# SyncE fetches ten side tiles per layer, with byte offsets worked out in the setup

## The chip, the cores and the metric

The kernel runs on one core of a Trainium2 chip. The metric is the time of one execution on the device in microseconds (us). Beside three timed executions there is one profiled execution, from which all rows below come. Engines are named as the profile names them: PE is TensorE, DVE is VectorE, ACT is ScalarE, POOL is GpSimd, SP is SyncE; SPq is SP's own sequence of instructions, which are not counted as busy time.

## The reference

Four graph layers run one after the other on a graph of 6250 nodes and 100000 edges, sorted by destination; every layer reads rows of 128 numbers by the source of an edge and adds them up by its destination.

```python
edge_index = jnp.stack([src, dst])
h = jnp.maximum(_layernorm(x, axis=-1), 0.0)
x = x + _L0_gnn_ref(h, src, dst, weight, b)              # mean of (h @ W)[src], self loops
h = jnp.maximum(_layernorm(x, axis=-1), 0.0)
x = x + _L1_gnn_ref(h, W1, W2, b1, b2, edge_weight, src, dst)   # sum of h[src] * edge_weight
h = jnp.maximum(_layernorm(x, axis=-1), 0.0)
x = x + _L2_gnn_ref(h, edge_attr_128, ..., src, dst)     # sum of (h @ Wn)[src] * net(edge_attr)
h = jnp.maximum(_layernorm(x, axis=-1), 0.0)
x = x + _L3_gnn_ref(h, edge_index, ...)                  # 4-head attention over the sources
```

## The kernel before

**Tiles and groups.** The sorted edges are cut into 782 tiles of 128, four tiles to a group, 196 groups. For every layer the node rows stand in a table in device memory (T0 with 129 numbers a row, T1 and T2 with 128, T3 with 133). An edge loop (`edge_loop` for layers 0 to 2, its own code for layer 3) brings the source rows of each tile into one of 32 places of the ring `work`, which holds eight groups, and PE multiplies each place by a mask that DVE builds from the destinations, which sums them by node.

**Who fetches.** POOL gathers a tile with one indirect DMA (`gather_groups`, L683), one table row to each partition. Before group g it waits until group g - 8 is free (L680). In seven groups of a layer, listed in `SIDE_AT`, POOL gathers three tiles only; the fourth, a **side tile**, is SP's. SP fetches its 128 rows one at a time over earlier groups: `fetch_rows` (L715 to L731) loads five row numbers into registers (L640 in `numbers`), issues one small DMA for each from the table to a side buffer (L728), and, when 64 numbers are used up, asks for the piece of 64 after next (`read_sources`, L713). Two groups after a side tile's last row, `place_rows` (L737) copies the buffer into the ring. At L728 a register holds the row's number; SP turns it into an offset with one FUSED_REGOPS, which multiplies by the row's length and by four.

**What sets the order on SP.** `relay_groups` is SP's loop, one turn a group, written out without branches. In turn n it loads four numbers of `closing` if n is a multiple of four (L640), then in `ready(n + ahead)` waits for the gathers of a later group and tells PE, DVE or ACT that they are there (L762), then fetches rows, then waits until PE or its like has used group n and raises the count that frees it for POOL (L781). In layer 2 it also loads a pair of groups of the edge network's output every second turn (L752). So an instruction that is slow in the row fetches holds up both signals behind it: L781, for which POOL waits, and the next turn's L762.

**Beside it.** ACT, PE and DVE work through the edge network in layers 0 and 1, node updates come at the end of each layer, and the setup (x, constants, the first table T0, the control tables made from sorted destinations by DVE at L402 to L513) comes before layer 0's loop. In the setup, SP's stores of T0 are L357, and L516 stores a table of windows.

Of the kernel before, what the change touches and what calls it, by code (L numbers as in the profile page):

```python
# [6 lines left out]

F32 = mybir.dt.float32
I32 = mybir.dt.int32
ALU = mybir.AluOpType  # L10
ACT = mybir.ActivationFunctionType
AX = mybir.AxisListType
ENG = mybir.EngineType

N, E, D = 6250, 100000, 128
P = 128
# [10 lines left out]
QUAD = 4  # L27
# [1 line left out]
GROUPS = -(-E // GRP)  # L29
TILES = GROUPS * QUAD  # L30
RING = 8
SIDE, SIDE_PER, SIDE_READ = 7, 5, 64
SIDE_BEGIN = [-(-(P * j) // SIDE_PER) for j in range(SIDE + 1)]
SIDE_AT = [SIDE_BEGIN[j + 1] + RING + 2 for j in range(SIDE)]
BANKS = 2
# [22 lines left out]
ROW3 = HEADS + D + 1  # L58
# [47 lines left out]
def need(engine, *marks):  # L106

    for sem, value in marks:
        engine.wait_ge(sem, value)


def build(nc, a, out):
    with ExitStack() as ctx:
# [6 lines left out]
        def dram(name, shape, dt=F32):  # L120
            return nc.dram_tensor("d_" + name, shape, dt, kind="Internal").ap()

        pe, dve, act, pool, sp = nc.tensor, nc.vector, nc.scalar, nc.gpsimd, nc.sync
        V = Lane(dve, sem("v_done"))
# [41 lines left out]

        winB, slotB = sb("winB", [1, TABB], I32), sb("slotB", [1, TABB], I32)
        needB, closingB = sb("needB", [1, TABB // QUAD], I32), sb("closingB", [1, GROUPS], I32)
# [4 lines left out]
        rn = sb("rn", [P, 2, NT])  # L173
# [20 lines left out]
        T0, T1, T2, T3 = dram("T0", [NP, D + 1]), dram("T1", [NP, D]), dram("T2", [NP, D]), dram("T3", [NP, ROW3])  # L194
        scores = dram("scores", [NP, 2 * HEADS])
        windows_b = dram("windows_b", [1, TABB])


        ld_c, ld_w = Load("ld_c"), Load("ld_w")
# [14 lines left out]
        ld_t = Load("ld_t")  # L214
# [13 lines left out]

        ld_g.add(sp.dma_start(lastg, a["lastg"]))
        ld_g.add(sp.dma_start(lastrow, a["lastrow"]))  # L230
        ld_c.add(sp.dma_start(cst[:], a["consts"]))
        steps = hT[:, 4 * TABB:5 * TABB]
        ld_c.add(sp.dma_start(steps, a["steps"].to_broadcast([P, TABB])))
        ld_t.add(sp.dma_start(rawdst, a["dsts"]))
        ld_t.add(sp.dma_start(idx, a["idx"]))
        ld_l.add(sp.dma_start(lastb, a["lasts"].to_broadcast([P, ROWS])))
        ld_t.add(sp.dma_start(wgt, a["wgt"]))
        for k, name in enumerate(("w0", "w1", "w2", "wnT", "we1T", "we2T", "wf1T", "wf2T")):
# [144 lines left out]
        st_0, dv0, nm0 = Load("st_0"), {}, {}  # L383
# [52 lines left out]
        V.did(dve.tensor_scalar(closing2[:], closing2[:], 1, None, ALU.arith_shift_right))  # L436
        V.did(dve.tensor_scalar(ctl3[:, 0:STEPS + 1, 3], slot_s, float(QUAD * ACC3), None, ALU.mult))
        need(dve, ld_t.mark)
        tables = V.did(dve.tensor_copy(dstf, rawdst))


# [82 lines left out]
        prepared = V.did(dve.memset(bcol[:, 7:8], 0.5))  # L524
# [113 lines left out]
        def numbers(engine, view, values, lo, top):  # L638

            _, v = nc.values_load_multi_w_load_instructions(  # L640
                view, engines=[engine], min_val=lo, max_val=top,
                skip_runtime_bounds_check_because="made on the chip from the sorted dst, bounded by the staircase's shape")
            assert len(v) == values
            return v
# [53 lines left out]
        def side_rows(layer, j):  # L698

            lo, width = (MLP + 11 * GRP, ACC3) if layer < 3 else (0, ROW3)  # L700
            return (acc if layer < 3 else work[:, RING * QUAD * ROW3:])[:, lo + j % 2 * width:lo + (j % 2 + 1) * width]

        def side_sources(layer, c):

            row = acc[0:1, NT * ACC3:XC] if layer < 3 else work[0:1, (RING * QUAD + 2) * ROW3:]
            return row[:, c % 2 * SIDE_READ:(c % 2 + 1) * SIDE_READ].bitcast(I32)
# [3 lines left out]

        def read_sources(layer, c):

            sp.dma_start(side_sources(layer, c), a["sides"][0:1, c * SIDE_READ:(c + 1) * SIDE_READ])\  # L713
                .then_inc(s_src[c % 2], 16)

        def fetch_rows(layer, table, n):

            width = table.shape[1]
            for c in range(SIDE_READS):
                lo, hi = [min(max(SIDE_PER * m - SIDE_READ * c, 0), SIDE_READ) for m in (n, n + 1)]  # L720
                if lo == hi:
                    continue
                if lo == 0:
                    sp.wait_ge(s_src[c % 2], 16 * (SIDE_READS // 2 * layer + c // 2 + 1))
                found = numbers(ENG.SP, side_sources(layer, c)[:, lo:hi], hi - lo, 0, N - 1)
                for r, row in zip(range(c * SIDE_READ + lo, c * SIDE_READ + hi), found):
                    j, p = divmod(r, P)
                    sp.dma_start(side_rows(layer, j)[p:p + 1, 0:width], table[bass.ds(row, 1), :])\  # L728
                        .then_inc(s_row[layer][j % 4], 16)
                if hi == SIDE_READ and c + 2 < SIDE_READS:  # L730
                    read_sources(layer, c + 2)  # L731
# [824 lines left out]
            return over  # L1556


        over = edge_loop(0, T0, [st_0.mark, ld_t.mark], [st_0.mark, ld_t.mark, prepared, tables])
        for e in (pe, dve, act, pool, sp):  # L1560
            need(e, *over)

# [1 line left out]
        over = edge_loop(1, T1, [st_1.mark], [st_1.mark, cleared[0]])  # L1564
# [15 lines left out]
        over = edge_loop(2, T2, [st_2.mark], [st_2.mark, cleared[1]])  # L1580
# [451 lines left out]
```

## Time and profile before

| | us |
|---|---|
| median of three timed runs | 5319.39 |
| lowest, highest | 5316.58, 5325.49 |
| span of the profiled execution | 5348.7 |

The profiled execution's own time isn't among the three; its span, from the first to the last instruction, is 29 us longer than their median. The span holds four edge loops, from about 85 to 1275 us, 1310 to 2530, 2595 to 3830 and 3920 to 5215, and shorter stretches between and around them. A window of the span given as 150 to 1200 is a stretch of layer 0's loop in which all that is described above repeats group by group.

### The profile page before, as it was taken

The numbers are of one execution on the slowest core, as the hardware profiler recorded it, in microseconds if no ns is written. First come the engines' busy times: TensorE is split into PE (matmuls) and PEld (weight loads), VectorE is DVE, ScalarE is ACT, GpSimd is POOL, SyncE is SP. The second block draws the span as 40 slices with busy tenths as digits, with TensorE's granted clock in tenths as the row PEclk, the third lists the DMA queues.
The fourth block names the chain that finished last, engine by engine and source line by source line (L and its number), as shares of the span: only waits on it lengthen the run. The fifth ranks groups of instructions, "written<-read, shape, count | busy, mean of one in ns | idle before, by whom it ended". The sixth has DMA issues, their size and how long they took to land. (4 is left out here: it accounts for less than half of the span.)

```text
span 5348.7 us, 68713 instructions
## 1 busy us (share of the span) xinstructions
PE 2667.0 (50%) x13316; PEld 2230.9 (42%) x13316; DVE 2614.4 (49%) x7231; ACT 1816.7 (34%) x4182; POOL 2997.4 (56%) x3172
## 2 busy tenths in 40 slices
PE   2555555544455555555333333333555555555557
PEld 1444444443344444445333333333444444444446
DVE  3333333333455555546333333333456667767678
ACT  2333333311233333312111111112345555656555
POOL 4556565555556555556355565555345555555553
PEclk7777777766777777767655565656667777767779
DMA  5333333322233333322222222223272111111110
GB/s 113 93 98 100 89 99 97 91 66 54 81 98 91 97 97 90 98 66 56 73 80 82 86 86 82 85 82 87 70 135 48 42 42 42 42 42 42 42 44 25
DMA packets 241787, 405.91 MB, mean 76 GB/s; under 512 B 67715, under 2 KB 140572, under 8 KB 241373
## 3 DMA queue, kind: packets, MB, share of 16 engines
q0 software_dynamic: 99456, 206.27, 15.7%
q10 hardware_dynamic: 74432, 122.18, 8.2%
q1 hardware_dynamic: 67484, 73.06, 4.8%
q8 instruction: 123, 2.02, 0.2%
q14 instruction: 292, 2.38, 0.1%
HBM read 331.63 MB, written 67.78 MB: 75 GB/s over the span
## 5 line engine op out<-in xcount | busy, mean ns | idle before, releaser
L683 POOL DMA_INDIRECT t_work<-d_T,t_tabG x3100 | 2926.8, 944 | 2183.9 <-SPq L781 1098.6
L1367 PE MATMUL ps<-t_work,t_acc 128*128 x2592 | 493.7, 355 | 647.6 <-SPq L762 459.1
L1367 PEld LDWEIGHTS ps<-t_work,t_acc 128*128 128x128 f32 x2592 | 440.9, 258 | 727.1 <-issue 726.7
L1428 DVE TENSOR_TENSOR t_acc<-t_acc,ps 128x128 f32 (+1 forms) x732 | 210.6, 288 | 914.8 <-remote 459.0
L1804 PE MATMUL ps<-t_work,t_hT 128*128 x1960 | 394.5, 363 | 339.0 <-ACT t_hT L1792 157.9
L1417 DVE TENSOR_TENSOR t_hT<-t_work,ps 128x512 f32<-128x512 f32 x244 | 167.2, 685 | 763.7 <-ACT ps L1504 615.0
L1804 PEld LDWEIGHTS ps<-t_work,t_hT 128*128 128x128 f32 x1960 | 337.5, 260 | 406.1 <-issue 406.1
L1367 PE MATMUL ps<-t_hT,t_acc 128*128 128x128 f32 x1296 | 275.2, 399 | 434.6 <-DVE t_acc L1428 313.0
L1504 ACT COPY ps<-t_acc 128x512 f32 x244 | 140.5, 588 | 1022.2 <-SPq L762 723.9
L596 ACT ACTIVATE t_acc<-ps,t_bcol 128x1024 f32<-128x1024 f32 x98 | 109.1, 1113 | 1079.6 <-DVE ps L609 587.4
L1367 PEld LDWEIGHTS ps<-t_hT,t_acc 128*128 128x128 f32 x1296 | 259.5, 306 | 452.6 <-DVE t_hT L1417 295.8
L1367 PE MATMUL ps<-t_work 128*128 x1312 | 247.8, 354 | 323.9 <-SPq L762 212.0
L1714 DVE TENSOR_TENSOR t_hT<-t_work,ps 128x128 f32<-128x128 f32 x980 | 270.9, 281 | 282.6 <-issue 178.6
L1367 PEld LDWEIGHTS ps<-t_work 128*128 128x128 f32 x1312 | 222.6, 258 | 364.6 <-issue 364.5
L1814 DVE SCALAR_TENSOR_TENSOR t_acc<-t_acc,t_hT,ps 128x129 f32 x980 | 336.9, 344 | 68.4 <-remote 56.3
L1726 PE MATMUL ps<-t_cst,t_hT 128*128 128x128 f32 x980 | 204.3, 344 | 249.0 <-DVE t_hT L1714 123.8
L563 PE MATMUL ps<-t_acc,t_wts 128*128 128x512 f32 x392 | 283.1, 864 | 78.8 <-DVE t_acc L602 41.1
L1777 ACT ACTIVATE t_hT<-t_hT 128x128 f32<-128x128 f32 x980 | 310.0, 390 | 0.0
L1792 ACT COPY t_hT<-ps 128x512 f32<-128x512 f32 x245 | 144.3, 589 | 464.7 <-remote 373.1
L572 PE MATMUL ps<-t_wts,t_acc 128*128 128x128 f32 x1568 | 265.4, 341 | 41.0 <-DVE t_acc L617 23.5
L1734 ACT ACTIVATE t_hT<-ps,t_hT 128x128 f32<-128x128 f32 x980 | 273.9, 359 | 32.4 <-remote 31.0
L572 PEld LDWEIGHTS ps<-t_wts,t_acc 128*128 128x128 f32 x1568 | 257.9, 257 | 45.4 <-issue 45.3
(189 smaller groups left out, 4469.0 us busy)
## 6 DMA issues: line engine op xcount, KB each, us to landing
d_edge_net<-t_acc ACTq DMA_DIRECT2D x98, 512.0 KB
t_acc<-d_edge_net SPq DMA_DIRECT2D x98, 512.0 KB
t_work<-d_T,t_tabG POOLq DMA_INDIRECT x3100
t_acc<-in_edge_attrT ACTq DMA_DIRECT2D x96, 512.0 KB
t_acc<-d_T SPq DMA_DIRECT2D x1792, 0.5 KB
t_acc<-d_T SPq DMA_DIRECT2D x896, 0.5 KB
t_work<-d_T SPq DMA_DIRECT2D x896, 0.5 KB
t_acc<-d_T ACTq DMA_DIRECT2D x12, 790.1 KB
```

What stands on the lines that cost most here:

```text
L563: last = pe.matmul(ps[:, 4 + h, :], WE1, ein[n % 2][:, h * GRP:(h + 1) * GRP], start=True, stop=True)
L572: last = pe.matmul(ps[:, 6 + k // QUAD, k % QUAD * D:(k % QUAD + 1) * D], sp1[:, k * P:(k + 1) * P], WE2, start=True, stop=True)
L683: pool.indirect_dma_start(out=work[:, at:at + width], out_offset=None, in_=table, in_offset=bass.IndirectOffsetOnAxis(ap=idx[:, g * QUAD + ...
L1367: last = pe.matmul(sums(layer, s, width), masks[s % MASKS][:, k, :], rows_k, start=(k == 0), stop=(k == QUAD - 1))
L1417: dve.tensor_tensor(out=scaled_rows[s % MASKS].rearrange("p (k d) -> p k d", k=QUAD), in0=ring[:, bass.ds(slot, QUAD * ACC3)].rearrange("p ...
L1428: dve.tensor_tensor(out=o, in0=o, in1=sums(layer, s, width), op=ALU.add).then_inc(e_acc[layer], 1)
L1714: ins = dve.tensor_tensor(out=tw[n % 2][:, k * P:(k + 1) * P].rearrange("p (h n) -> p h n", h=HEADS), in0=slots3[:, bass.ds(slots[k], HEAD ...
L1726: last = pe.transpose(ps[:, PT + n % 2, k * P:(k + 1) * P], tw[n % 2][:, k * P:(k + 1) * P], ident)
L1734: last = act.activation(ex[n % 3][:, k * P:(k + 1) * P], ps[:, PT + n % 2, k * P:(k + 1) * P], ACT.Identity, bias=ads[:, QUAD * n + k:QUAD ...
L1777: last = act.activation(e, e, ACT.Exp, bias=run[:, 0, c0 + k:c0 + k + 1], scale=1.0)
L1804: last = pe.matmul(out_of(n, k), pw[n % 2][:, k * P:(k + 1) * P], slots3[:, bass.ds(slots[k] + HEADS, ACC3)], start=True, stop=True)
L1814: dve.scalar_tensor_tensor(out=o, in0=o, scalar=corr[:, n % RINGB, k:k + 1], in1=out_of(n, k), op0=ALU.mult, op1=ALU.add).then_inc(s_add, 1)
```

## The change

The number of side tiles goes from seven to ten a layer (`SIDE`), and SP fetches seven rows a group for five (`SIDE_PER`). `SIDE_AT` goes from 36, 62, 87, 113, 138, 164, 190 to 29, 47, 65, 84, 102, 120, 138, 157, 175, 193. The row numbers are no longer read from the input but from a small table in device memory, `side_at`, with a line for each row length: in the setup DVE multiplies the numbers by the length of a row in bytes, three times, and SP stores the products. At the row fetch the table is seen as bytes, and the register holds the offset itself.

```diff
-SIDE, SIDE_PER, SIDE_READ = 7, 5, 64
+SIDE, SIDE_PER, SIDE_READ = 10, 7, 64
...
+        side_at = dram("side_at", [3, SIDE * P], I32)
...
+        side_tab = rn[:].rearrange("p j t -> p (j t)")[:, 0:4 * SIDE].bitcast(I32)
+        ld_k, st_k = Load("ld_k"), Load("st_k")
...
         ld_t.add(sp.dma_start(idx, a["idx"]))
+        ld_k.add(sp.dma_start(side_tab[:, 0:SIDE], a["sides"]))
...
         need(dve, ld_t.mark)
+        need(dve, ld_k.mark)
+        for k, width in enumerate((D + 1, D, ROW3)):
+            m_side = V.did(dve.tensor_scalar(side_tab[:, (k + 1) * SIDE:(k + 2) * SIDE], side_tab[:, 0:SIDE],
+                                             float(4 * width), None, ALU.mult))
+        need(sp, m_side)
+        st_k.add(sp.dma_start(side_at.rearrange("k (p j) -> p k j", j=SIDE),
+                              side_tab[:, SIDE:4 * SIDE].rearrange("p (k j) -> p k j", j=SIDE)))
...
-            sp.dma_start(side_sources(layer, c), a["sides"][0:1, c * SIDE_READ:(c + 1) * SIDE_READ])\
+            k = (layer + 1) // 2
+            sp.dma_start(side_sources(layer, c), side_at[k:k + 1, c * SIDE_READ:(c + 1) * SIDE_READ])\
...
-            width = table.shape[1]
+            row = 4 * table.shape[1]
+            table_b = table.rearrange("n w -> (n w)").unsqueeze(0).bitcast(U8)
...
-                found = numbers(ENG.SP, side_sources(layer, c)[:, lo:hi], hi - lo, 0, N - 1)
-                for r, row in zip(range(c * SIDE_READ + lo, c * SIDE_READ + hi), found):
+                found = numbers(ENG.SP, side_sources(layer, c)[:, lo:hi], hi - lo, 0, (N - 1) * row)
+                for r, at in zip(range(c * SIDE_READ + lo, c * SIDE_READ + hi), found):
                     j, p = divmod(r, P)
-                    sp.dma_start(side_rows(layer, j)[p:p + 1, 0:width], table[bass.ds(row, 1), :])\
+                    sp.dma_start(side_rows(layer, j)[p:p + 1, :].bitcast(U8)[:, 0:row], table_b[:, bass.ds(at, row)])\
...
-        over = edge_loop(0, T0, [st_0.mark, ld_t.mark], [st_0.mark, ld_t.mark, prepared, tables])
+        over = edge_loop(0, T0, [st_0.mark, ld_t.mark], [st_0.mark, ld_t.mark, st_k.mark, prepared, tables])
```

The order of SP's instructions at the start of layer 0's loop, one turn of `relay_groups`. ISA is the FUSED_REGOPS of the profile, t_acc holds the row numbers and receives the rows, d_T is the table; before:

```order
L640 TENSOR_LOAD t_closing
L640 TENSOR_LOAD t_acc
L728 ISA
L728 DMA t_acc<-d_T 1x129
L728 ISA
L728 DMA t_acc<-d_T 1x129
L728 ISA
L728 DMA t_acc<-d_T 1x129
L728 ISA
L728 DMA t_acc<-d_T 1x129
L728 ISA
L728 DMA t_acc<-d_T 1x129
```

The same turn and the three behind it after the change (L652 is the old L640, L742 the old L728; 516 are bytes):

```order
L652 TENSOR_LOAD t_closing
L652 TENSOR_LOAD t_acc
L742 DMA t_acc<-d_T 1x516 x7
L652 TENSOR_LOAD t_acc
L742 DMA t_acc<-d_T 1x516 x7
```

The register instruction before each row's DMA is gone, and seven DMAs stand in a turn in place of five.

Where a piece of 64 numbers ends within a turn on SP, before:

```order
L640 TENSOR_LOAD t_acc
L728 ISA
L728 DMA t_acc<-d_T 1x129
L713 DMA t_acc<-in_sides 1x64
L640 TENSOR_LOAD t_acc
```

And after:

```order
L652 TENSOR_LOAD t_acc
L742 DMA t_acc<-d_T 1x516
L726 DMA t_acc<-d_side_at 1x64
L652 TENSOR_LOAD t_acc
L742 DMA t_acc<-d_T 1x516 x6
```

Such a turn has two loads of numbers and a read of the piece after next, as before; there are more of them.

SP's setup after the change, from its last store of T0 to its first read of numbers, with what each waits for:

```order
L362 DMA d_T<-t_acc 128x129 [waits g_done,a_done] x2
L449 DMA d_side_at<-t_rn 128x3x10 [waits v_done]
L528 DMA d_windows_b<-t_acc 1x1024 [waits v_done]
L558 DMA t_acc<-in_edge_attrT 128x1024 [waits v_done]
L558 DMA t_acc<-in_edge_attrT 128x1024
L726 DMA t_acc<-d_side_at 1x64 [waits v_done,st_k,ld_t,st_0]
```

The store of `side_at` (L449) is new, ahead of the store of windows (the old L516), and the first read waits for it too.

## Rows read from the trace of the kernel before

Rows that begin with a line's name say: instruction and its tiles, how many, duration in ns (least/median/most), first and last start in us. Those of the windows say: stretch and its length, busy us and count of PE, PEld (weight loads), DVE, ACT and POOL, granted TensorE clock, share of the DMA engines, GB/s. Those of the timeline say: start, duration, engine and instruction, and in brackets the idle time before it and what ended it.

**Rows 1.** The page: busy times, and by line the chain that ended last.

```profile
PE 2667.0 (50%) x13316; PEld 2230.9 (42%) x13316; DVE 2614.4 (49%) x7231; ACT 1816.7 (34%) x4182; POOL 2997.4 (56%) x3172
...
SPq L728 8%; SPq L640 3%; PE ps L1804 1%; SPq L762 0%; DVE t_acc L1814 0%; PE ps L1944 0%; ACT t_hT L1777 0%; SPq L781 0%; DVE t_acc L1913 0%; ACT t_hT L1734 0%; DVE t_x L1976 0%; DVE t_dev L302 0%; PE ps L1726 0%; PE ps L1785 0%
```

**Rows 2.** Windows, one steady stretch in each of the four edge loops.

```profile
150.00:1200.00 1050.00, 563.84 (x2696) 456.24 (x2696) 387.92 (x661) 329.79 (x313) 625.83 (x664) 0.73 0.34 92
1450.00:2450.00 1000.00, 558.43 (x2644) 452.28 (x2645) 519.27 (x835) 316.78 (x327) 593.62 (x630) 0.73 0.31 89
2750.00:3750.00 1000.00, 361.15 (x1683) 335.41 (x1681) 333.35 (x642) 130.89 (x235) 589.87 (x626) 0.60 0.29 84
4000.00:5100.00 1100.00, 619.88 (x3268) 504.75 (x3268) 775.00 (x3303) 650.30 (x2253) 606.93 (x644) 0.76 0.20 44
```

**Rows 3.** Waits of POOL, layer 0's stretch, then layer 3's: us, times, longest.

```profile
POOL t_work L683 <- SPq L781: 212.9, 69, 4.9
...
POOL t_work L683 <- SPq L781: 313.9, 111, 5.0
```

**Rows 4.** Timeline of POOL in layer 0, idle before in brackets.

```profile
1019.97 0.94 POOL L683 DMA_INDIRECT t_work<-d_T,t_tabG  x1 [2.30 <-SPq L781]
1021.22 0.94 POOL L683 DMA_INDIRECT t_work<-d_T,t_tabG  x1 [0.30 <-issue]
...
1033.71 0.94 POOL L683 DMA_INDIRECT t_work<-d_T,t_tabG  x1 [0.30 <-issue]
1039.46 0.94 POOL L683 DMA_INDIRECT t_work<-d_T,t_tabG  x1 [4.81 <-SPq L781]
```

**Rows 5.** SP's instructions by line, layer 0's stretch; last row layer 3's L781.

```profile
L728 SPq FUSED_REGOPS  x838: 1/37/1413, 150.9 to 1197.5; - x168
L728 SPq MOVE t_acc<-d_T x838: 1/29/1452, 151.1 to 1198.9; - x168
L728 SPq DMA_DIRECT2D t_acc<-d_T x838: 2/225/1396, 151.8 to 1199.0; - x168
...
L781 SPq EVENT_SEMAPHORE  x167: 2/17/1422, 154.4 to 1193.4; - x167
...
L781 SPq EVENT_SEMAPHORE  x163: 2/17/751, 4001.6 to 5097.6; - x163
```

**Rows 6.** SP's loads of numbers, layer 0's stretch.

```profile
L640 SPq TENSOR_LOAD <-t_acc x179: 3/1072/3222, 149.7 to 1193.5; - x179
...
L640 SPq TENSOR_LOAD <-t_closing x42: 3/485/1564, 154.4 to 1179.8; - x42
```

**Rows 7.** Row fetches in POOL's pause, then beside its gathers.

```profile
L728 SPq MOVE t_acc<-d_T x4: 3/29/29, 1037.1 to 1038.3; - x4
...
L728 SPq FUSED_REGOPS  x5: 5/37/707, 1023.8 to 1027.8; - x5
...
L728 SPq DMA_DIRECT2D t_acc<-d_T x5: 3/28/702, 1024.2 to 1028.5; - x5
```

**Rows 8.** The last row fetch of layer 0, and the semaphore instructions behind it.

```profile
L728 SPq DMA_DIRECT2D t_acc<-d_T x1: 6/6/6, 1226.5 to 1226.5; - x1
...
L762 SPq EVENT_SEMAPHORE  x3: 251/714/720, 1227.0 to 1229.4; - x3
```

**Rows 9.** Reads of row-number pieces and placements, whole span.

```profile
L713 SPq DMA_DIRECT2D t_acc<-in_sides x42: 3/236/729, 81.9 to 3610.5; - x42
...
L737 SPq DMA_DIRECT2D t_work<-t_acc x21: 3/483/712, 286.6 to 3775.2; - x21
```

**Rows 10.** Setup: VectorE's L437, SP's L516 and L713, landing of L357.

```profile
L437 DVE TENSOR_SCALAR t_ctl<-t_acc x1: 366/366/366, 45.0 to 45.0; 1x245 int32<-1x245 int32 x1
...
L516 SPq DMA_DIRECT2D d_windows_b<-t_acc x1: 252/252/252, 77.8 to 77.8; - x1
...
L713 SPq DMA_DIRECT2D t_acc<-in_sides x2: 238/243/248, 81.9 to 82.2; - x2
...
DMA to landing us min/median/max: 5.1/8.2/9.5
```

More of the change, by code:

```diff
@@ L9 @@
 I32 = mybir.dt.int32
+U8 = mybir.dt.uint8
 ALU = mybir.AluOpType
@@ L2007 @@
         "lastg": lastg.reshape(2, P).T, "lastrow": lastg[:GROUPS].reshape(1, GROUPS),
-        "sides": np.concatenate([src[QUAD * g + QUAD - 1] for g in SIDE_AT]).reshape(1, SIDE * P),
+        "sides": np.concatenate([src[QUAD * g + QUAD - 1] for g in SIDE_AT]).reshape(P, SIDE),
         "idx": src[:TILES].T, "dsts": dst[:TILES].T, "wgt": weight[:TILES].T,
```

## The prediction

> **What bounds the kernel now.** I read the page's busy line and its chain first [rows 1]. No engine is busy more than 56% of the span (POOL), while the chain that ended last carries two lines of SP's queue on top: L728, the row fetches, and L640, the loads of numbers into registers. Next, the four stretches in which an edge loop runs steadily [rows 2]: POOL is busy 0.55 to 0.60 of each, PE at most 0.56, VectorE 0.70 in the last. So the question is what POOL waits for. Between gathers it stops for 0.30 us ("issue"), and on top of that it waits for SP's L781, the semaphore that frees a ring group: 212.9 us of layer 0's 1050 us and 313.9 of layer 3's 1100 [rows 3]. The timeline shows the shape: gathers follow each other every 1.25 us, so a group of four needs 5.0 us; then a pause of 2.3 to 4.8 us ended by L781 [rows 4].
>
> Is SP late because it waits, or because it works? The view of waits names no wait of SP in these stretches, and L781 was passed 167 times in 1050 us [rows 5], **6.29 us a group**, against POOL's 5.0. SP's sequencer never rests: SP bounds the edge loops, and 1.29 us a group is what POOL loses to it.
>
> **What SP's 6.29 us are.** A group has one load of five row numbers (median 1.07 us), every fourth group one of `closing` (0.485, so 0.12 a group) [rows 6], two semaphore instructions (0.017 each, with the step between instructions some 0.1 together) and five rows of three instructions each: FUSED_REGOPS 0.037, MOVE 0.029, DMA 0.225, 0.29 together [rows 5]. What a row takes is another matter. While POOL paused, MOVEs began at 1037.1 to 1038.3, three steps in 1.2 us: **0.40 us a row**. While gathers ran, FUSED_REGOPS began at 1023.8 to 1027.8, four steps in 4.0: **1.0 us a row**, with stalls of some 0.7 us or twice that in any of the three [rows 5, 7]. The stalls hit semaphore instructions too: three at L762 took 0.25, 0.71 and 0.72 us from 1227.0 on, after layer 0's last row fetch at 1226.5 [rows 8]. So with gathers in flight SP runs at less than half its speed, and in the pause at full speed. Clean work per group: 5 x 0.40 + 1.07 + 0.12 + 0.1 = 3.29 us. The pause takes 1.29 of it, so 2.00 was done in the 5.0 us of gathers, a rate of 0.40.
>
> **The change part by part.**
> (1) FUSED_REGOPS goes from each row; DMA and its MOVE stay (the built program still has a MOVE behind each row's DMA), and the bytes of a row are the same. Clean, that saves 0.037 and its step: 0.40 less 0.29 is 0.11 for three steps, so 0.037 + 0.037 = 0.07. The bounds of a whole row's saving are 0.037 (its bare duration) and a third of a stalled row, 0.33.
> (2) Two more rows a group: 7 x 0.33 = 2.31 clean for 5 x 0.40 = 2.00. +0.31.
> (3) The load brings seven numbers for five. Five take 1.07, 0.21 each: +0.43. By the row of four numbers it would be 0.12 each, +0.24; by the step from four numbers to five, 0.59 each, +1.17 [rows 6]. I take 0.43, from the load that is lengthened itself. The Trainium skill, "Runtime: NRT & Kernel Launch", section "Instruction fetch mechanics", gives about 200 ns for each register that such a load fills; that would make +0.40, and it speaks against this change in the same measure as the row does.
> (4) Per layer there are 200 loads of row numbers for 191 (more rows straddle the 64-number pieces), 20 reads of a piece for 14 at 0.23 us, ten placements for seven at 0.48 [rows 9]: clean some 9 x 0.25 + 6 x 0.23 + 3 x 0.48 = 5 us, or 0.03 a group. The 0.25 is what a load costs beside its values, estimated as 0.485 less two values of 0.12.
> (5) Rows are fetched in 183 groups a layer for 180: three more groups pay the pause of 1.29 us, +4 us a layer.
> (6) Three gathers fewer a layer, 3 x 1.25 = 3.75 us. POOL isn't the bound: SP lacks the 0.40 x 3.75 = 1.5 us of work that it did beside them, so 2.2 us a layer are gained. Were POOL the bound, all four layers would gain 15 us: that is the most the fewer gathers can give.
> (7) Setup: a small load, three VectorE instructions of ten columns, a store. They stand behind L437, which starts at 45.0; SP's next store, L516, starts only at 77.8 and the first read of the table at 81.9 [rows 10]. 32 us cover a store that the 5.1 to 9.5 us landings of the T0 stores bound from above [rows 10]. Nothing; without cover at most 10 us, once.
>
> **The sum, and how stalls are shared.** Clean work per group becomes 3.29 + 0.31 + 0.43 + 0.03 = 4.06 us. What remains open is how much of it SP gets done in the 5.0 us of gathers, and three readings of the stalls give three times.
> (a) Each instruction pays its own stall. Before, 15 + 1.25 + 2 = 18.25 instructions have 0.18 us of clean work each, and at the rate of 0.40 take 0.45: 0.27 of stall each. Afterwards 14 + 1.3 + 2 = 17.3 have 0.235 and take 0.505, so 9.9 pass in 5.0 us and 7.4 are left for the pause: 1.74 us, +0.45 a group.
> (b) Instructions pass at a fixed pace when gathers run, 11.1 in 5.0 us, and a longer one hides its stall. 6.2 are left at 0.235: 1.46 us, +0.17.
> The truth should lie between. For (b) speaks that the long load shows a median of 1.07 although most loads run beside gathers; for (a), that a DMA of 0.225 shows stalls of its own, up to 1.396 [rows 5]. I take the middle, **+0.31 us a group**. Over 183 groups and four layers that is +227; (5) and (6) add 4 x 2: +235. Layer 3 has a longer group, 1100/163 = 6.75 us [rows 5], so a larger share of pause, and I take the same step for it. The profiled span of 5348.7 becomes 5584; the median of the timed runs is 0.55% below that span, and carrying the difference gives 5319 + 235, about **5550 us**, 4.3% slower. With (a) alone 5650, with (b) alone 5450. A TENSOR_LOAD at either bound moves the sum by -70 or +290 us, worked the same way.
>
> **The rivals.**
> *Stalls take a share of time* (slower still). If SP simply runs at 0.40 of its speed beside gathers whatever it executes, 2.00 us are done there and 2.06 left: +0.77 a group, +572 us with (5) and (6), 5890. For it: the rate is the simplest reading of 0.40 against 1.0 us a row. Against it: bare register instructions with 0.037 of work stall as long as DMAs do.
> *FUSED_REGOPS feeds the stalls* (faster). Without it SP alternates between two kinds of instruction in a row and not three. If that halved the stall of every other instruction, from 0.27 to 0.13, 0.235 + 0.13 = 0.37 each, 13.5 pass in 5.0 us, 3.8 are left: 0.89 us of pause, -0.40 a group, about -290: 5030. It turns into a gain once the stall of the others falls below some 0.19, by 30%. For it: row instructions stall in any position. Against it: in the pause the same sequence runs without stalls, so the sequence alone causes none; and the semaphore instructions, with no register arithmetic near, stalled as well [rows 8].
> *Nothing to see.* If the loads' two further numbers cost 0.12 each and stalls go by (b), the step is +0.1 or less, and a stall or two less per group brings it to zero: 5310 to 5370.
> *The change doesn't do what it says*: the order shows FUSED_REGOPS gone from all rows, so only the MOVE could differ; I give it nothing.
>
> **How the numbers follow.** Forecast 5550 (between 5420 and 5700): 0.55. By share of time, 5760 and up: 0.15. Faster, through weaker stalls: 0.20, half of it above 5180. No difference: 0.10, of which some 0.06 within 0.2%, about what a measurement of this kernel can tell from no change. Range 5180 to 5780: it leaves out half of the faster case and most of the share-of-time case, 2 in 10 together. Faster 0.22, same 0.06, slower 0.72.
>
> **What the profile of the changed kernel would show.** Right: no FUSED_REGOPS at the row fetch and 5120 rows; the free signal passed every 6.5 to 6.8 us in layer 0; the loads of seven numbers at 1.4 to 1.6 us; POOL's waits for the free signal up from 213 us to some 260 in the same stretch; POOL's own step still 1.25 us. Wrong: the free signal at 6.2 us or below with rows at 0.5 us beside gathers (the stalls shrank); at 7 us or above (share of time); or waits of SP for PE or for landed gathers in the steady stretches, which would mean that SP no longer bounds.

## The result: 5352 us for 5320, and the profile after

The changed kernel takes 5352.4 us (median of 4 runs, 5349.2 to 5356.2); the kernel before took 5319.8 beside it (4 runs, 5316.6 to 5325.5). The ratio is 1.0063, with a 95% interval of 1.005 to 1.0077: slower, by 0.6% where 4.3% were forecast. The profiled run took 5356.2 us, its span is 5354.9.

The page of the kernel after, busy times, the chain by line, and the gathers; they answer to [rows 1]:

```profile
PE 2722.2 (51%) x13316; PEld 2286.6 (43%) x13316; DVE 2615.0 (49%) x7234; ACT 1820.7 (34%) x4182; POOL 2987.2 (56%) x3160
...
SPq L742 33%; SPq L652 19%; SPq L776 1%; SPq L795 1%; SPq L766 1%; PE ps L1381 1%; POOL t_work L695 0%; PE ps L1818 0%; DVE t_acc L1828 0%; ACT t_acc L314 0%; DVE t_acc L1927 0%; PE ps L1958 0%; SPq L726 0%; DVE t_x L1990 0%
...
L695 POOL DMA_INDIRECT t_work<-d_T,t_tabG x3088 | 2914.5, 944 | 2208.2 <-SPq L795 1122.7
```

SP's instructions by line in layer 0's stretch of 1050 us (count, least/median/most in ns, first and last start), as in [rows 5] and [rows 6]; L742 was L728, L652 was L640, L795 was L781:

```profile
L742 SPq MOVE t_acc<-d_T x1162: 2/29/1414, 151.5 to 1200.0; - x194
L742 SPq DMA_DIRECT2D t_acc<-d_T x1161: 2/228/1397, 151.6 to 1199.7; - x194
...
L652 SPq TENSOR_LOAD <-t_acc x182: 3/1466/3450, 149.0 to 1194.7; - x182
...
L795 SPq EVENT_SEMAPHORE  x165: 2/17/1411, 154.2 to 1192.5; - x165
```

POOL's waits in layer 0's stretch and in layer 3's (us, times, longest), as in [rows 3]:

```profile
POOL t_work L695 <- SPq L795: 220.3, 69, 5.3
...
POOL t_work L695 <- SPq L795: 313.3, 119, 5.4
```

FUSED_REGOPS is gone, 1161 rows pass in 1050 us where 838 did, and the load of seven takes 1.47 us. Yet the free signal comes 165 times for 167: 6.36 us a group for 6.29. POOL waits for it as often as before, 69 times, 3.2 us each for 3.1; in layer 3 nothing moved either, 313.3 us for 313.9. From start to start in the trace, layer 0's stretch, a row took 0.89 us of SP before (DMA 0.39, FUSED_REGOPS 0.25, MOVE 0.25) and 0.60 after (0.36 and 0.24). So five rows took 4.47 us, seven take 4.18; the loads of numbers took what the rows gave back, 1.57 us a group for 1.29.

### The profile page after: what moved, and what is told of

Read it like the earlier page. It is cut to its first block, busy times and chain, and to the rows that moved or that the text cites. A ratio compares the mean times of both kernels' runs of the same rounds, so it can differ in the third digit from the quotient of the medians.

```text
span 5354.9 us, 68270 instructions
## 1 busy us (share of the span) xinstructions
PE 2722.2 (51%) x13316; PEld 2286.6 (43%) x13316; DVE 2615.0 (49%) x7234; ACT 1820.7 (34%) x4182; POOL 2987.2 (56%) x3160
## 4 chain that ended last, share of the span: by engine, by line
SPq 56%; issue 30%; DVE 4%; another core or an unknown queue 3%; PE 3%; ACT 2%; POOL 1%; DVEq 0%; DMA 0%; ACTq 0%; POOLq 0%
SPq L742 33%; SPq L652 19%; SPq L776 1%; SPq L795 1%; SPq L766 1%; PE ps L1381 1%; POOL t_work L695 0%; PE ps L1818 0%; DVE t_acc L1828 0%; ACT t_acc L314 0%; DVE t_acc L1927 0%; PE ps L1958 0%; SPq L726 0%; DVE t_x L1990 0%
## 5 line engine op out<-in xcount | busy, mean ns | idle before, releaser
L1818 PE MATMUL ps<-t_work,t_hT 128*128 x1960 | 409.8, 373 | 246.1 <-issue 130.5
L1818 PEld LDWEIGHTS ps<-t_work,t_hT 128*128 128x128 f32 x1960 | 349.6, 268 | 315.0 <-issue 315.0
L1740 PEld LDWEIGHTS ps<-t_cst,t_hT 128*128 128x128 f32 x980 | 137.0, 177 | 381.7 <-DVE t_hT L1728 296.1
L584 PE MATMUL ps<-t_wts,t_acc 128*128 128x128 f32 x1568 | 276.3, 351 | 6.1 <-issue 5.5
```

The lines of the kernel that those rows point to most:

```text
L584: last = pe.matmul(ps[:, 6 + k // QUAD, k % QUAD * D:(k % QUAD + 1) * D], sp1[:, k * P:(k + 1) * P], WE2, start=True, stop=True)
L1740: last = pe.transpose(ps[:, PT + n % 2, k * P:(k + 1) * P], tw[n % 2][:, k * P:(k + 1) * P], ident)
L1818: last = pe.matmul(out_of(n, k), pw[n % 2][:, k * P:(k + 1) * P], slots3[:, bass.ds(slots[k] + HEADS, ACC3)], start=True, stop=True)
```

## The experiments

**Two kinds of chip.** Where a run lands decides more than any edit here. On three chips the kernel before takes 5262 to 5331 us (below: chips A; the 5320 beside the result is of this kind), on three others 4183 to 4187 (chips B). Every ratio is against the kernel before on the same chip.

| run | edit | chip | us | before | ratio, 95% interval |
|---|---|---|---|---|---|
| e1 | five rows, byte offsets | B | 4187.6 | 4186.9 | 1.000, 0.999 to 1.001 |
| e2 | seven rows, FUSED_REGOPS | B | 4296.0 | 4186.9 | 1.026, 1.024 to 1.028 |
| e3 | no side tiles | B | 4216.4 | 4186.9 | 1.007, 1.005 to 1.009 |
| e4 | the change, aligned loads | B | 4176.7 | 4186.9 | 0.997, 0.996 to 0.999 |
| e5 | the change again | A | 5278.7 | 5262.2 | 1.003, 1.002 to 1.005 |
| e6 | before, for its trace | A | 5282.2 | 5262.2 | one run |
| e7 | as e1 | A | 5292.8 | 5324.4 | 0.993, 0.991 to 0.996 |
| e8 | as e2 | A | 5708.7 | 5324.4 | 1.073, 1.070 to 1.075 |
| e9 | as e4 | A | 5352.4 | 5324.4 | 1.006, 1.004 to 1.008 |
| e10 | as e3 | A | 5246.2 | 5324.4 | 0.985, 0.983 to 0.988 |
| e11, e12 | the change, 2 and 4 idle instructions a gather | B | 4169.9, 4171.1 | 4183.3 | 0.997, 0.995 to 0.998 (both) |
| e13 | before, 2 of them | B | 4182.2 | 4183.3 | 1.000, 0.999 to 1.001 |
| e14, e15 | the change, 6 and 8 | A | 5331.4, 5359.1 | 5331.0 | 1.001 and 1.005, 0.9995 to 1.002 and 1.003 to 1.007 |
| e16 | before, 6 | A | 5253.1 | 5331.0 | 0.986, 0.984 to 0.988 |
| e17 | the change, gathers of 64 rows | B | 4046.5 | 4183.2 | 0.967, 0.966 to 0.969 |
| e18 | the change, gathers of 64 columns | B | 4168.5 | 4183.2 | 0.997, 0.996 to 0.998 |

**The change taken apart** (T1: each instruction brings its own stall; T2: a fixed pace or a share of time). e1 keeps the byte offsets and goes back to five rows:

```
-SIDE, SIDE_PER, SIDE_READ = 10, 7, 64
+SIDE, SIDE_PER, SIDE_READ = 7, 5, 64
```

> The changed kernel with seven side tiles and five rows a turn, as before, so only the offsets in bytes are left of the change. Theory 1 (SP's instructions bound the edge loops): a row takes 0.30 us less than before, 1.5 us of SP's time a group, of which the coupling with POOL leaves 0.6 to 0.8 us: groups of 5.5 to 5.7 us, 4740 to 4900 us in all. Theory 2 (the group's 6.3 us are set elsewhere, by landings or by what uses the ring, and SP only fills them, which is why the group stayed at 6.3 us with the change): 5300 to 5330.

e2 keeps ten tiles and seven rows, and lets SP multiply again (the table then holds row numbers, multiplied by 1.0 in the setup):

```
-sp.dma_start(side_rows(layer, j)[p:p + 1, :].bitcast(U8)[:, 0:row], table_b[:, bass.ds(at, row)])
+sp.dma_start(side_rows(layer, j)[p:p + 1, 0:width], table[bass.ds(at, 1), :])
```

> The changed kernel with ten side tiles and seven rows a turn, but with row numbers in the registers and the multiplication back at each row: the other half of the change alone. Theory 1: 0.30 us more for each of seven rows, at least a third of it on the group: 6.9 to 7.5 us a group, 5750 to 6200 us. Theory 2: about 5350.

e3 has no side tile (SIDE = 0): POOL gathers every tile, SP fetches no row.

> No side tiles: POOL gathers all 782 tiles of a layer, SP only passes signals. Theory 1: POOL's 5.0 us a group become the bound, less 1.3 us for 180 groups in four layers, plus 28 gathers at 1.25 us: 4400 to 4500 us. Theory 2: 5300 to 5400.

e4 is the change with each group's seven numbers in a slot of eight:

```
+SIDE_SLOT = 8
-found = numbers(ENG.SP, side_sources(layer, c)[:, lo:hi], hi - lo, 0, (N - 1) * row)
+found = numbers(ENG.SP, side_sources(layer, c)[:, lo:lo + many], many, 0, (N - 1) * row)
```

> The changed kernel with the seven offsets of a turn placed in eight, so that each load begins at a multiple of 32 bytes and no turn straddles a piece. Theory 1: a load of seven takes 0.9 to 1.1 us where it took some 1.5, and 17 fewer loads a layer: 0.2 to 0.5 us less a group, 5000 to 5200 us. Theory 2: 5340 to 5360.

All four landed on a chip B, where no expectation in us could hold. What they show is the kernel without stalls. SP's row instructions in e2, from 150 to 1200 us (on a chip B that is layer 0's loop to about 1050 and the start of layer 1's):

```profile
L741 SPq FUSED_REGOPS  x1327: 37/37/37, 150.0 to 1199.6; - x190
L741 SPq MOVE t_acc<-d_T x1327: 29/29/29, 150.0 to 1199.7; - x190
L741 SPq DMA_DIRECT2D t_acc<-d_T x1327: 224/225/1018, 150.1 to 1199.8; - x190
```

The longest of 1327 FUSED_REGOPS takes 37 ns; in [rows 5] it was 1413. Gathers run as densely here, or denser, so gathers alone cause no stall: it takes the chip as well. In e1 POOL is the bound, its idle time being mostly its own 0.30 us ("issue") between gathers; in e2 SP is, with 54% of the chain. The gathers of e1, then e2's chain:

```profile
L695 POOL DMA_INDIRECT t_work<-d_T,t_tabG x3100 | 2935.9, 947 | 1054.9 <-issue 904.2
```

```profile
SPq L741 29%; SPq L652 25%; POOL t_work L695 8%; DMA t_work<-d_T,t_tabG 2%; SPq L765 1%; DVE t_acc L1827 1%; PE ps L1380 1%; ACT t_acc L314 0%; DVEq L652 0%; PE ps L1957 0%; PE ps L575 0%; DVE t_acc L1926 0%; SPq L726 0%; DVE t_x L1989 0%; DVE ps L1414 0%
```

Seven rows with FUSED_REGOPS need 5.2 us a group in e2 (from the starts, layer 0), over POOL's 5.0; without it they fit. There the edit does what a reader of the code would hope.

**The same on chips A.** First the change itself and the kernel before once more:

> The changed kernel itself, unaltered, beside the kernel before on one chip. On the chip of the first four experiments the kernel before takes 4187 us, where it took 5320 beside the first run of the change. Theory A: what differs is the stalls of SyncE's instructions beside the gathers (a FUSED_REGOPS 256 ns in the trace of before, 76 ns in that of e2_7rows_regops). Where the kernel before takes near 4190, the change takes 4175 to 4205: GpSimd's 1.25 us a gather is the bound, twelve gathers fewer are worth up to 15 us, and loads of seven that are not aligned give back part of it. Where it takes near 5320, the change takes 5340 to 5365 again, a ratio of 1.005 to 1.008. Theory B (SyncE is the bound in either case, and the change adds the same work to a group): a ratio of 1.005 to 1.01 in both.

> The kernel before, unaltered, for its trace on this chip. Where it takes near 4190 us: theory A expects FUSED_REGOPS 0.07 to 0.08 us, MOVE 0.06 to 0.07 and the issue of a row's DMA 0.26 to 0.30 us from one instruction to the next beside the gathers, a group of 5.0 us, and SyncE waiting in the first loop. Theory B expects groups over 5.1 us, with GpSimd waiting for SyncE's free signal at one group in two or more. Where it takes near 5320: 0.25, 0.25 and 0.39 us as in the first trace.

The chip was an A: 1.003, a little under what was expected, and a FUSED_REGOPS of 0.24 us from start to start. Then e1 to e4 again, all on one chip A:

> The kernel of e1 once more (five rows and seven side tiles as before, byte offsets, so FUSED_REGOPS is all that goes), wanted on a chip where the kernel before takes near 5260 us. There its row takes 0.89 us of SyncE's time beside gathers (0.40 DMA, 0.24 MOVE, 0.24 FUSED_REGOPS) and in the change 0.60. Theory P (each instruction brings its own stall of some 0.17 us): 5 x 0.60 + 1.21 of loads + 0.6 of the rest = 4.8 us a group, under GpSimd's 5.0, so the free signal comes in time and the time falls to 4300 to 4500 us. Theory S (the gathers set the number of stalls, whatever SyncE executes): only the clean 0.07 to 0.09 a row go, 0.4 us a group, 4900 to 5000. Theory R (a stall merely moves to the next instruction and fills the time): 5230 to 5270. Where the kernel before takes 4187 again: 4180 to 4195.

> The kernel of e2 once more (ten side tiles and seven rows as in the change, FUSED_REGOPS as before), on the same chip as e7. Theory P: 7 x 0.89 + 1.6 of loads + 0.6 = 8.4 us a group for 6.2, some 6700 to 6900 us. Theory S: two more rows at their clean 0.42 and 0.35 more of loads, 7.4 us a group, 6100 to 6250. Theory R: 5300 to 5600. Where the kernel before takes 4187: 4290 to 4300 again.

> The kernel of e4 once more (the change, with the seven numbers of a group in a slot of eight, so that every load begins at a multiple of 32 bytes and no group needs two loads), on the same chip as e7. Its loads should take some 1.4 us for 1.6 a group. If SyncE's clean work counts in full (P and S): 5278 - 0.2 x 730 = 5100 to 5180 us. If stalls fill what the load leaves (R): 5240 to 5280. Where the kernel before takes 4187: 4174 to 4180 again.

> The kernel of e3 once more (no side tiles: GpSimd gathers every tile, SyncE fetches no rows), on the same chip as e7. If all that differs between the two chips is SyncE's stalls, the time is that of the other chip, 4210 to 4260 us, where the kernel before takes 5262, so that the row fetches cost 1000 us here. If the gathers or the other engines are slower here as well: 4400 us or more.

P (each instruction brings its stall) and S (gathers set the number of stalls) fall with e7. Five of SP's instructions a group are gone, a row takes 0.79 us for 0.89, and the kernel gains 0.7%; R (a stall moves on and fills the time) is nearest. e8 came out between R and S, and e9 (5352) above both of its ranges: aligned loads gave nothing. The run that decides is e10: SP fetches nothing, its queue idles, and the time falls by 1.5% only. Had SP's stalls been all that the two kinds of chip differ in, e10 would have come at 4210 to 4260 us; it took 5246, and e3, the same kernel on a chip B, 4216. Free signals in the stretch and POOL's waits for them, e10, e7, then e8:

```profile
L782 SPq EVENT_SEMAPHORE  x177: 17/17/17, 151.3 to 1187.5; - x177
...
POOL t_work L684 <- SPq L782: 166.8, 52, 6.1
```

```profile
L795 SPq EVENT_SEMAPHORE  x175: 2/17/1398, 155.5 to 1192.9; - x175
...
POOL t_work L695 <- SPq L795: 188.9, 65, 4.4
```

```profile
L794 SPq EVENT_SEMAPHORE  x157: 1/17/707, 150.1 to 1198.9; - x157
...
POOL t_work L695 <- SPq L794: 291.1, 90, 6.2
```

POOL waits 3.2, 2.9 and 3.2 us on average in the three, 3.1 in the kernel before and 3.2 in the change. The mean wait hardly depends on what SP has to do; what changes is how often it comes: 52, 65, 69, 69 and 90 times in e10, e7, before, the change and e8.

Who is late in e10? TensorE's timeline (start, duration, what, idle before):

```profile
994.90 1.39 PE L1368 MATMUL ps<-t_work,t_acc 128*128 x11
997.11 0.27 PE L1368 MATMUL ps<-t_work,t_acc 128*128 x1 [0.81 <-issue]
997.81 0.27 PE L1368 MATMUL ps<-t_work,t_acc 128*128 x1 [0.43 <-issue]
999.24 0.38 PE L1368 MATMUL ps<-t_work,t_acc 128*128 x1 [1.16 <-issue]
1001.37 0.60 PE L1368 MATMUL ps<-t_work,t_acc 128*128 x2 [1.75 <-issue]
1010.70 1.19 PE L564 MATMUL ps<-t_acc,t_wts 128*128 128x512 f32 x1 [8.74 <-DVE t_acc L603]
```

Eleven matmuls pass in 1.4 us, and then they come one at a time, on steps of 0.7, 1.4 and 2.1 us: SP's steps, on another engine. In this stretch SP waits in its turn; where the profile names who ended a wait of L782 it is TensorE (33 times of 87), and "remote" means that it names nobody:

```profile
SPq L782 <- remote: 731.4, 54, 23.7
SPq L782 <- PE ps L573: 106.8, 20, 6.9
```

The 8.74 us in front of the last matmul are more than a stall of TensorE. From 1001.97 to 1008.53 us the trace has no instruction of any engine but POOL, whose gathers go on; its last one before the pause ends at 1005.43, and the others go on 3.1 us later. In e10's layer 2 such standstills are longer. A window of 20.3 us (counts of PE, weight loads, DVE, ACT and POOL), then the first instructions of VectorE and POOL behind it:

```profile
3009.90:3030.20 20.30, 0.00 (x0) 0.00 (x0) 0.00 (x0) 0.00 (x0) 12.21 (x13) 0.57 0.25 71
3030.36 0.71 DVE L1429 TENSOR_TENSOR t_acc<-t_acc,ps 128x128 f32 x2 [21.64 <-remote]
3033.14 0.95 POOL L684 DMA_INDIRECT t_work<-d_T,t_tabG  x1 [7.38 <-SPq L782]
```

VectorE waited for the semaphore of a matmul that began at 3009.53; the trace has the signal at 3030.24. Whether the matmul or its signal was late, it doesn't tell. Counted in the trace, stretches of over 5 us without any instruction but POOL's, SP's included, are 23 of layer 0's 1050 us (189 us in all), 10 of 1000 us of layer 1 (91 us), 34 of 1000 us of layer 2 (546 us) and none in layer 3, whose 6.80 us a group stay unexplained. Of the 33 in layers 0 and 1, 23 end 2.9 to 3.2 us after the last gather of a run ends. e3, the same kernel on a chip B, has none in any layer. So in layers 0 to 2 of e10 it is the run of gathers that holds up the rest, and POOL then waits for what it held up. The kernel before and the change have no such stretch over 1.5 us: there SP always gets an instruction through.

**When the stalls come.** POOL's pauses in the kernel after (idle time in brackets), then SP's row fetches from 1007.2 to 1010, 1014 to 1020 and 1020 to 1022.7 us:

```profile
1007.43 0.94 POOL L695 DMA_INDIRECT t_work<-d_T,t_tabG  x1 [3.56 <-SPq L795]
1020.01 0.94 POOL L695 DMA_INDIRECT t_work<-d_T,t_tabG  x1 [2.90 <-SPq L795]
```

```profile
L742 SPq MOVE t_acc<-d_T x5: 29/29/29, 1008.4 to 1009.8; - x5
...
L742 SPq DMA_DIRECT2D t_acc<-d_T x6: 3/694/711, 1013.8 to 1018.9; - x6
...
L742 SPq MOVE t_acc<-d_T x4: 29/29/29, 1021.3 to 1022.4; - x4
```

A run of gathers starts at 1007.4. For 3 us more SP runs clean, then its DMAs take 0.7 us each. The next run starts at 1020.0, and again SP is clean at first. Over layer 0's stretch of the kernel before, from the starts in the trace, 35% of the FUSED_REGOPS stall (over 0.6 us from start to start) from 2.75 us behind a run's start to 2.75 us behind its end (the run's shadow), and 1% at other times. Within a run the share grows: of its MOVEs and FUSED_REGOPS (over 0.5 us, loops of layers 0 and 1) at most 1 in 100 stall in the first 2 us, some 3 in 10 in the fifth and sixth, some 6 in 10 from the seventh on. Loads of five numbers take 0.89 us on average within the shadow and 1.10 outside, so they show no stall on top of their own time, though single ones take up to 3.2.

The pauses fit to this. Counted from the starts in the same stretch; a pause is the step between two gathers less 1.25 us, where that is over 0.95 us:

| kernel on a chip A | gathers per pause | usual run, and its median pause |
|---|---|---|
| e10, no rows | 13.4 | 16 gathers, 3.5 us |
| e7, five rows, bytes | 10.9 | 12 gathers, 3.5 us |
| before | 8.6 | 8 gathers, 2.6 us; 12 gathers, 4.1 us |
| the change | 8.1 | 8 gathers, 2.6 us |
| e8, seven rows, FUSED_REGOPS | 7.1 | 8 gathers, 3.4 us |

A usual pause takes 0.18 to 0.34 of the run ahead of it. By the free signals a group takes 5.93 us in e10, 6.00 in e7, 6.29 before, 6.36 in the change and 6.69 in e8: SP's rows matter, but far less than their own time. That suggests a limit on the gathers themselves (theory B: they pile up, the pile stalls every sequencer, and it drains only while POOL stops).

Two things in the traces narrow B down. First, not every queue stalls. In layer 0's stretch steps of over 1.0 us between two weight loads of one line, which no kernel on a chip B shows, number 41 in e10 and 24 in e7, all in the shadow of a run, and none before, in the change and in e8, whose runs are shorter. POOL's own 167 semaphore instructions before take 0.02 us at most, and so do ScalarE's. Second, what piles up isn't the gathers' data. By the packets in the traces from 150 to 1000 us, a gather's first one starts 1.64 us behind the gather's start and its last one ends 2.2 us behind it (medians), for the first gather of a run as for the eighth, at most 5.3 us before and 5.3 in e10; on a chip B it is 1.65, 2.2 and 5.2 us (e13). Nor is it the fetching of instructions by its number: SP's row instructions before stall 572 times in the stretch, with 46 packets on one of the two instruction queues and 26 on the other. And no slower clock of TensorE explains a standstill in which it runs nothing; the granted clock was about 0.70 on chips A and 0.78 on chips B.

**Slower gathers.** To tell B from C (each gather brings its own stalls) and D (gathers have no part in it), POOL got semaphore instructions that nobody waits for behind each gather. The list `s_pace` has two; e12 runs over it twice (`s_pace * 2`), e14 and e16 three times, e15 four times:

```
                         .then_inc(GATHERED[g % RING], 16)
+                    for s in s_pace:
+                        pool.sem_inc(s, 1)
```

> The change, with two semaphore instructions on GpSimd behind every gather that nobody waits for, so that a gather takes some 1.38 us for 1.25 and a group at least 5.5 for 5.0. Wanted where the kernel before takes 5260 to 5320 us. The traces so far show SyncE's stalls of 0.7 us only from 3 us after a run of gathers begins to 3 us after it ends, and more of them the longer the run lasts. Theory B (gathers that follow each other faster than some 6.1 us a group pile up, and the pile is what stalls the sequencers): slower gathers mean fewer stalls, the share of row instructions over 0.6 us falls from 0.30 to under 0.2, and the time stays within 1% of the change's own, 5270 to 5400. Theory C (each gather brings its own stalls, whatever went ahead): the share stays at 0.3 and the group at 6.3 or more, 5300 to 5450. Theory D (SyncE's stalls have nothing to do with gathers, and GpSimd's 5.0 us hides nothing): the pause stays 1.3 us on top of 5.5, 5600 to 5750. Where the kernel before takes 4187: 4450 to 4650, since GpSimd is the bound.

> The same with four such semaphore instructions behind every gather: some 1.5 us a gather, 6.0 a group. Theory B: at that pace nothing piles up, the share of row instructions over 0.6 us falls to 0.1 or less, GpSimd hardly waits for the free signal, and a group takes 6.1 to 6.3 us: 5200 to 5400 us, about the same as without the pace although a gather takes a fifth longer. Theory C: the share stays near 0.3, the group at 6.3 to 6.6, 5300 to 5550. Theory D: 1.3 us of pause on top of 6.0, 6000 to 6150. Where the kernel before takes 4187: 4850 to 5050.

> The kernel before with the two semaphore instructions of e11. SyncE has 0.6 us less clean work a group than in the change. Theory B: fewer stalls and less work, so the group follows GpSimd at 5.6 to 6.1 us, 5000 to 5300 us, at least 1% under e11. Theory C: 6.2 to 6.4 us a group, 5300 to 5400. Theory D: 5600 to 5700. Where the kernel before takes 4187: 4450 to 4650.

These three ran on a chip B, and the gathers didn't slow down: the median step stayed 1.25 us, so the times are those of the bare kernels. The four instructions of e12 didn't fit into the 0.30 us between two gathers, as the next expectation has it; most of them ran while a gather was busy. That gives the change its time on such a chip: 4169.9 for 4183.3, 13 us faster, for its twelve gathers fewer (e3, with 28 more, is 29 us slower).

> The change with six semaphore instructions behind every gather on GpSimd. Four of them (0.078 us each in the trace of e12) fitted into the 0.30 us that GpSimd leaves between gathers, so six should make a gather 1.41 us and a group 5.6. Where the kernel before takes 5260 to 5320 us: theory B (gathers that pile up stall the sequencers) expects the share of SyncE's row instructions over 0.5 us to fall from 0.30 to under 0.2 and the time to stay within 1% of the change's own, 5270 to 5400; theory C (each gather brings its own stalls) a share of 0.3, 5300 to 5450; theory D (nothing of SyncE's work is hidden in the longer gathers) 5600 to 5750. Where the kernel before takes 4187: 3096 x 0.16 = 490 more than 4170, some 4600 to 4700.

> The same with eight semaphore instructions: 1.57 us a gather, 6.3 a group. Where the kernel before takes 5260 to 5320 us: theory B expects a share of stalls of 0.1 or less, hardly a wait of GpSimd for the free signal, and 5350 to 5500 us; theory C a share near 0.3 and 5450 to 5650; theory D 6100 or more. Where the kernel before takes 4187: 3096 x 0.31 = 970 more than 4170, 5050 to 5200.

> The kernel before with the six semaphore instructions of e14. SyncE has 0.6 us less clean work a group than in the change. Where the kernel before takes 5260 to 5320 us: theory B expects the group to follow GpSimd at 5.7 to 6.1 us, 5000 to 5300 us, and under e14 by 1% or more; theory C 6.2 to 6.4 us a group, 5250 to 5400; theory D 5600 to 5750. Where the kernel before takes 4187: 4600 to 4700.

On a chip A the times fell where B had them, but by no proof of B: POOL's queue ran ahead of its gathers, the median step between gathers stayed 1.25 us in all three, and of SP's MOVEs 28% and 23% still stalled in e14's and e15's shadow, for 31% in e5, where B wanted under 20% and 10%. e14's and e16's times suit C as well. What they do show: the stalls hit POOL's queue too, once it has many instructions beside its gathers (in e15 259 of its 5345 semaphore instructions take over 0.5 us). Its added instructions, and its waits, in e15:

```profile
L702 POOLq EVENT_SEMAPHORE  x5182: 2/17/732, 149.8 to 1199.4; - x200
...
POOL t_work L697 <- issue: 409.4, 630, 4.1
POOL t_work L697 <- SPq L799: 29.7, 17, 2.4
```

They take up to 0.73 us, where e12's, on a chip B, show:

```profile
L702 POOLq EVENT_SEMAPHORE  x3300: 17/17/17, 150.2 to 1199.9; - x195
```

In e15 POOL waits 30 us for SP in place of 220, and 409 us for its own queue, in place of 196. In e14 to e16 the runs became shorter (5.2 to 6 gathers, 1.8 us of pause), and in e15 the group is 6.36 us again, 165 free signals. With 32 more instructions a group on POOL the change takes as long as without them (1.005 for 1.003 to 1.006), and the kernel before with 24 more is 1.4% faster.

**Rows or bytes.** e17 gathers 64 of 128 rows behind the first eight groups, e18 64 of 129 columns:

> The change with every gather on GpSimd behind the first eight groups cut to its first 64 of 128 rows (the other rows keep what an earlier group left there, so the sums are others and the work of all other engines is the same). Where the kernel before takes 5260 to 5340 us: if the rows that pile up are what stalls the sequencers (theory B, by rows), the share of SyncE's row instructions over 0.5 us falls from 0.30 to under 0.1 and the group from 6.3 us to SyncE's or GpSimd's bound of 4.2 to 5.0, so 4000 to 4400 us; if each gather brings its stalls by its number alone (C), share and time stay, 5250 to 5350; if neither gathers nor their rows matter (D), 5300 as well, with the stalls also outside the shadow of the gathers. Where the kernel before takes 4187: 4000 to 4170, by what a gather of 64 rows takes on GpSimd.

> The change with every gather behind the first eight groups cut to the first 64 of its 129 columns, all 128 rows (from a view of the table with rows of 64, so the sums are others). The number of rows is the same, the bytes half. Where the kernel before takes 5260 to 5340 us: by rows (B) or by gathers (C) nothing changes, 5250 to 5360; if it is the bytes that pile up, the share of stalls falls to under 0.15 and the time to 4200 to 4700. Where the kernel before takes 4187: 4150 to 4180.

Both ran on a chip B and tell nothing of the stalls. There half the rows shorten a gather by 5% and the step by 4% (0.899 us for 0.945, a step of 1.20 for 1.25), half the bytes by nothing.

## Why the prediction was right in its sign and wrong in its size

- **"SP bounds the edge loops, and 1.29 us a group is what POOL loses to it": this step failed.** The views showed SP never at rest and POOL waiting for SP, and both are so. But without any row fetch POOL still loses 167 us of the 1050 to that wait (e10, for 213 before), or 0.94 us a group of the 1.27, and the kernel gains 1.5%. The engine waited for was busy because it was stalled, and with its work gone others were held up in its place: in e10 the whole core but POOL stands still for up to 20 us while gathers run. A sequencer full of stalls isn't full of work. Why runs of gathers do this on chips A stays open.
- **"What remains open is how much of it SP gets done in the 5.0 us of gathers": wrong question.** All three readings took a rate beside gathers and put the rest of SP's work into the pause. Against +0.77 us a group of clean work, as forecast, (a) gave +0.45, (b) +0.17, the sum +0.31; 165 signals for 167 are +0.08. From before to the change the median pause stayed 2.6 us and came after 8.1 gathers for 8.6, and the share of stalls shrinks as the work grows: 43 to 50% of the row instructions in the shadow in e7 (over 0.6 us, by kind), 36 to 41% before, 31% in the change (e5), 18 to 24% in e8. That the stalls give way to SP's work is what the prediction lacked.
- **Clean work 3.29 to 4.06 us: right in its parts.** FUSED_REGOPS was priced at 0.07 us a row; e2 has 0.076 for it from start to start, and its DMA takes 0.01 more than e4's. With stalls it took 0.25, within the 0.33 given as the bound, and five of these paid for the two further rows. The load of seven took 1.47 us for the 1.4 to 1.6 forecast, +0.39 to the load of five. (The Trainium skill, "Runtime: NRT & Kernel Launch", section "Instruction fetch mechanics", has some 200 ns a register: by that rule +0.40. For these two registers the trace agrees; four numbers in 0.48 us, and 0.59 more for the fifth, don't follow it.)
- **The rows that were read as stalls "beside the gathers" and none in the pause** [rows 7]: right, but 3 us late. The four MOVEs at 1037.1 to 1038.3 begin 2.4 us into a pause; so the delay, and the clean first microseconds of the next run, weren't seen.
- **(5), (6), (7)**: on a chip B the fewer gathers are worth 13 us, for the 15 given "were POOL the bound". On a chip A they can't be told from the rest. The setup cost 0.2 us: the store that was L516 starts at 78.0 for 77.8, the first read of numbers at 82.1 for 81.9.
- **The rivals.** Stalls as a share of time (5890) is out. "FUSED_REGOPS feeds the stalls" is out as well: removing it alone gains 0.7% on a chip A and nothing on a chip B, and the share of MOVEs that stall in the shadow rises, from 36 to 50% (e7). "Nothing to see", 5310 to 5370 at 0.10, held the time, though not by its mechanism.
- **Signs named ahead.** The free signal was to come every 6.5 to 6.8 us: 6.36. POOL's waits some 260: 220. POOL's own step stayed 1.25 us, as in [rows 4], and 1161 rows without FUSED_REGOPS are the change as described.

So on a chip A: FUSED_REGOPS away with five rows -0.7% (e7); seven rows and three more side tiles on top +1.0 to 1.3% (1.003 and 1.006 over 0.993); with FUSED_REGOPS left in, the seven rows cost +7.3% (e8). There more work of SP does cost time; that it then outgrows what the pauses leave is argued, not shown. No kernel here beats both everywhere: e7 beats them on a chip A and is even with the kernel before on a B, where the change leads by 0.3%; e16 (0.986) was tried on a chip A alone.

Open remains what the chips differ in, what it is of the gathers that piles up if it isn't their data, and what paces layer 3. That a run of gathers holds up the rest on a chip A is shown by e10 beside e3. That the same sets the pace of the kernel before and of the change rests on the pattern of pauses and stalls over nine kernels, no run having slowed or shortened the gathers on a chip A.

## What to carry to other kernels

When the engine that others wait for shows stalls in trivial instructions (a 29 ns MOVE that takes 700), don't price its work; take all of it away in one run first. If the time stays, something else paces the loop. And look at the pattern, not the sum: how long is a wait, how often does it come, what ran ahead of it, and what did all the other engines do meanwhile. A wait that stays near 3 us when the waited-for engine's work is taken away has another cause.

## What the runs showed of the hardware

- The same kernel took 5262 to 5331 us on three chips and 4183 to 4187 on three others. On the latter, SP's FUSED_REGOPS and MOVEs show no stall at all (0.04 us at most). SP's stalls aren't the whole difference: without its rows the kernel takes 5246 us on one kind and 4216 on the other (e10, e3).
- On the slower ones, SP's instructions stall in steps of 0.70 to 0.72 us from some 3 us behind the start of a run of indirect gathers to 3 us behind its end. TensorE's do so in e7 and e10, with the longest runs, and GpSimd's in e14 to e16. With SP idle, all engines but GpSimd stood still for up to 20 us (e10).
- Four semaphore instructions a gather on GpSimd, 0.078 us from one to the next, cost nothing on a chip B: they run while a gather is busy (e12, step 1.25 us).
- A gather of 64 rows costs GpSimd 0.90 us, one of 128 rows 0.95; 64 columns for 129 change nothing (e17, e18).
- Aligning the loads of numbers brought nothing, on either kind of chip (e4 0.997 as e11, e9 1.006 as the change).
